# An audio tower of 32 batches: both LayerNorms normalised by ScalarE with a scale and a bias per row, and the second one's variance asked for later in VectorE's step

## The reference

```python
x: (32, 256, 256); readout = x[:, :1]; other = x[:, 1:]            # 255 tokens of width 256
h = gelu(other @ W1 + readout @ W2 + b)                            # exact gelu
n = (h - mean(h)) / sqrt(var(h) + 1e-5)                            # LayerNorm 1, no affine
q, k, v = split(n @ qkv_w.T)                                       # 16 heads of 64
attn = softmax(q @ k.T / 8 + relative_position_bias)
h = h + concat_heads(attn @ v) @ o_w.T
m = (h - mean(h)) / sqrt(var(h) + 1e-5)                            # LayerNorm 2
gate, up = m @ (w_gate / 127).T, m @ (w_up / 127).T                # 768 columns each
h = h + (silu(gate) * up) @ (w_down / 127).T
```

## Time and profile before

| what | value |
|---|---|
| median of 3 runs | 1950.28 us (1949.91 to 1951.17) |
| the profiled execution's own time | 1951.19 us |
| its span, first to last instruction | 1949.3 us |
| one batch in the steady part | 57.80 us |
| PE, PEld, DVE, ACT, POOL busy | 95%, 88%, 82%, 73%, 51% of the span |
| mean granted TensorE clock | 0.988 of full speed |

### The profile page before, as it was taken

The page is one execution under the profiler, slowest core; times in us unless marked ns, Lnnn a source line. Parts: engine busy times, 40 slices in busy tenths (PEclk is TensorE's granted clock), DMA queues, the critical chain, the costliest instruction groups (busy, mean ns, idle before and its releaser), DMA issues.

```text
span 1949.3 us, 42778 instructions
## 1 busy us (share of the span) xinstructions
PE 1853.6 (95%) x15402; PEld 1725.0 (88%) x15402; DVE 1599.4 (82%) x4768; ACT 1422.6 (73%) x3810; POOL 990.2 (51%) x1295
## 2 busy tenths in 40 slices
PE   3699999999999999999999999999999999999995
PEld 1589999999999999999999999999999999999995
DVE  3488888888888888888888888888888888888884
ACT  5477777777777777777777777777777777777773
POOL 0255555455555555555555555555555545555553
PEclk9799999999999999999999999999999999999997
DMA  6100000000000000000000000000000000000000
GB/s 213 31 10 5 11 15 15 15 15 7 10 15 15 15 15 13 6 12 15 15 15 15 6 10 15 15 15 15 7 9 15 15 15 15 15 5 12 7 7 11
DMA packets 24885, 34.34 MB, mean 18 GB/s; under 512 B 2449, under 2 KB 17810, under 8 KB 24674
## 3 DMA queue, kind: packets, MB, share of 16 engines
q1 hardware_dynamic: 23906, 28.39, 4.9%
q0 software_dynamic: 768, 3.21, 0.4%
HBM read 23.17 MB, written 8.42 MB: 16 GB/s over the span
## 4 chain that ended last, share of the span: by engine, by line
PE 72%; DMA 12%; DVE 8%; issue 3%; ACT 2%; SPq 1%; POOL 0%; POOLq 0%; DVEq 0%
PE ps L484 41%; DMA out<-h 12%; PE ps L550 9%; PE ps L529 9%; PE ps L539 8%; PE ps L493 3%; PE ps L501 2%; DVE var_eps L805 1%; DVE stats L795 1%; DVE v L832 1%; DVE h L887 1%; ACT prob L716 1%; DVE heads L863 1%; DVE heads L861 1%; SPq L409 1%
## 5 line engine op out<-in xcount | busy, mean ns | idle before, releaser
L716 ACT ACTIVATE prob<-prob,neg_top 128x255 f32<-128x255 f32 x1024 | 508.3, 500 | 67.7 <-DVE neg_top L841 67.3
L442 POOL TENSOR_TENSOR prob<-prob,inv 128x510 f32<-128x510 f32 x512 | 520.3, 1037 | 68.1 <-DVE inv L855 63.9
L447 POOL CAST oT<-heads 128x256 fp32r<-128x256 f32 x256 | 105.9, 414 | 787.4 <-DVE heads L863 787.4
L484 PE MATMUL ps<-xnT,wqk 128*128 128x256 f32 x3072 | 411.6, 283 | 3.9 <-DVE qk L824 2.1
L850 DVE TENSOR_TENSOR pT<-ps,pT 128x512 fp32r<-128x512 f32 x512 | 352.0, 688 | 60.2 <-ACT pT L722 53.2
L484 PEld LDWEIGHTS ps<-xnT,wqk 128*128 128x128 f32 x3072 | 386.4, 189 | 12.2 <-DVE qk L824 2.9
L841 DVE CUSTOM_DVE_ANT_0 prob<-ps,bias 128x255 f32<-128x255 f32 x1024 | 369.6, 416 | 2.0 <-PE ps L529 1.9
L722 ACT ACTIVATE pT<-ps 128x512 fp32r<-128x512 f32 x512 | 302.8, 592 | 26.9 <-PE ps L539 25.0
L550 PE MATMUL ps<-pT,v 128*128 128x256 f32 x2048 | 295.0, 286 | 2.2 <-DVE pT L850 1.9
L550 PEld LDWEIGHTS ps<-pT,v 128*128 128x128 f32 x2048 | 265.1, 189 | 13.5 <-DVE pT L850 1.4
L539 PE MATMUL ps<-ident,prob 128*128 128x128 f32 x2048 | 265.4, 272 | 0.1
(11 more groups left out here) (93 smaller groups left out, 2479.5 us busy)
## 6 DMA issues: line engine op xcount, KB each, us to landing
xt<-x_cols SPq DMA_DIRECT2D x32, 256.0 KB, 2.7
r_rows<-readout_rows SPq DMA_DIRECT2D x32, 128.0 KB, 3.1
out<-h SPq DMA_DIRECT2D x32, 128.0 KB
out<-h SPq DMA_DIRECT2D x32, 127.0 KB
flipped<-bias_rows POOLq DMA_DIRECT2D x1, 3072.0 KB, 16.5
staged<-w_qk SPq DMA_DIRECT2D x8, 256.0 KB, 5.0
staged<-w_v SPq DMA_DIRECT2D x4, 256.0 KB, 7.3
staged<-w_o SPq DMA_DIRECT2D x4, 256.0 KB, 3.1
```

The lines of the kernel that those rows point to most:

```text
L442: pool.tensor_tensor(pr, pr, by, ALU.mult).then_inc(prob_done, 1)
L484: mm = pe.matmul(dst, lhs(a, k), rhs(b, k), start=(start and n == 0), stop=(stop and n == last), skip_group_check=skip)
L716: ex = act.activation(pr, pr, ACT.Exp, bias=neg_top[:, g % 2, hh, t:t + 1], scale=-1.0, accum_out=total[:, g % 2, hh, t:t + 1])
```

## The change

- `normalise` moves from VectorE to ScalarE. It becomes an activation with the function Identity, a scale per row (`rstd`) and a bias per row, for each of the two tiles. So for each LayerNorm two tensor_scalar of 128x256 leave VectorE and two activations of 128x256 come to ScalarE.
- The bias is minus the mean times `rstd`. VectorE negates the mean in place (a new tensor_scalar over 128x2 in `layer_var`, ahead of the one that adds epsilon). GpSimd multiplies it by `rstd`, behind its power, and writes the product over `var_eps` (a new tensor_tensor over 128x2, behind a wait for the power through the new semaphores `ln_pow`).
- On ScalarE `normalise(1, i-1)` stands in step 3 and `normalise(0, i+1)` in step 4, both between `heads_moved` and `probs_hi` of the first head of pair G-1.
- On VectorE `layer_var(1, i-1)` moves in step 3 from its place ahead of `values_lo` of group 2 to a place behind `probs_lo` of the second head, ahead of `queries_keys_lo`.
- The short description of the change also says that the fourth value group becomes the late user of step 3. The diff has no line of that kind: `V_EARLY`, `V_LATE`, `V_GROUP` and TensorE's order stay as they are.

```diff
@@ names of semaphores
+        ln_pow = [sem(f"ln{n}_pow") for n in (1, 2)]
@@ GpSimd, layer_norm
                     pool.wait_ge(ln_var[n], count(1, batch))
                     pool.tensor_tensor(rstd[:, n, :], var_eps[:, n, :], minus_half[:], ALU.pow
+                                       ).then_inc(ln_pow[n], 1)
+                    pool.wait_ge(ln_pow[n], count(1, batch))
+                    pool.tensor_tensor(var_eps[:, n, :], mean_var[:, n, :, 0], rstd[:, n, :], ALU.mult
                                        ).then_inc(ln_rstd[n], 1)
@@ ScalarE
+                def normalise(n, batch, src):
+                    act.wait_ge(ln_rstd[n], count(1, batch))
+                    for t in range(TT):
+                        ins = act.activation(normed[:, t, :], src[:, t, :], ACT.Identity,
+                                             bias=var_eps[:, n, t:t + 1], scale=rstd[:, n, t:t + 1])
+                    ins.then_inc(ln_done[n], 1)
@@ ScalarE, step
                     if pair(G - 2):
                         heads_moved(*pair(G - 2))
+                    if g == 3 and i > 0:
+                        normalise(1, i - 1, h1)
+                    if g == 4 and nxt:
+                        if prev:
+                            act.wait_ge(lnT_mm[1], count(1, i - 1))
+                        normalise(0, i + 1, token_tile(i + 1))
                     if pair(G - 1):
                         probs_hi(*pair(G - 1), 0)
 
                 gelu(0)
+                normalise(0, 0, token_tile(0))
@@ VectorE, layer_var
                     dve.wait_ge(ln_aggr[n], count(1, batch))
+                    dve.tensor_scalar(mean_var[:, n, :, 0], mean_var[:, n, :, 0], -1.0, None, ALU.mult)
                     dve.tensor_scalar(var_eps[:, n, :], mean_var[:, n, :, 1], EPS, None, ALU.add
                                       ).then_inc(ln_var[n], 1)
-
-                def normalise(n, batch, src):
...
@@ VectorE, step
-                    if g == 3 and i > 0:
-                        layer_var(1, i - 1)
                     if gu_at(G - 1, GU_LATE):
                         gating(*gu_at(G - 1, GU_LATE))
                     if v_at(G - 1, V_LATE):
                         values_lo(*v_at(G - 1, V_LATE))
                     if pair(G - 2):
                         probs_lo(*pair(G - 2), 1)
+                    if g == 3 and i > 0:
+                        layer_var(1, i - 1)
@@ VectorE, step, further down
-                    if g == 3 and i > 0:
-                        normalise(1, i - 1, h1)
...
-                    if g == 4 and nxt:
-                        if prev:
-                            dve.wait_ge(lnT_mm[1], count(1, i - 1))
-                        normalise(0, i + 1, token_tile(i + 1))
@@ VectorE, ahead of the steps
                 layer_var(0, 0)
-                normalise(0, 0, token_tile(0))
```

## The result

The changed kernel takes 1973.56 us (median of 4 runs, 1972.45 to 1974.01) against 1950.72 us for the kernel before in the same session: a ratio of 1.0116, with a 95% interval of 1.0099 to 1.0134. It is 1.2% slower. The forecast was 1973.5. The profiled span grew from 1949.3 to 1972.1 us, 22.8 against 23.2 in the sum of the prediction. The median of before was 1950.28 when the forecast was made and the runs of one kernel spread by 1.6 us, so an error of 0.1 us is finer than these times can show.

A forecast was written before the change was run, and what follows sets the result against it. TensorE, working 95% of the span, bounds the kernel, with one wait of 26.0 us for value group 2. Terms: 30 x 0.71 = 21.3, plus 0.2 and 1.7 for the ends, together 23.2: 1973.5 against 1950.28, range 1944 to 1982.

The forecast's parts named there:

- The bound and its cause: Step 3: TensorE waits 0.83 us ahead of values(i, 3), as VectorE's L805 waits for GpSimd; 26.0 us in all.
- The hold moves with the operation: Step 3: the wait for GpSimd moves from ahead of values(i, 3) to ahead of queries_keys_lo, starting at about 1013.20.
- The rival in which the hold vanishes: Step 3: neither 128x2 operation is held, queries_keys_lo starts near 1012.6; 0.30 us a batch, 1961; chance 10%.
- The price of a pair: Two normalising activations on ScalarE: 586 ns each, one holding the engine 0.49 us, a pair 0.98.
- The walk: Start times followed along VectorE and ScalarE through steps 3 and 4; gate_up(i-1, 1) and the next batch 0.71 us later.
- 4s - 1.25: Delay of a batch for s held by one normalisation: 0.71 us at 0.49, 0.39 at 0.41, 0 at 0.31.
- The ends: Both ends of the program, where LayerNorm's path is open: 0.85 us each, 1.7 for both.
- What I would have seen: Profile after: L832 wait gone, hold about 0.75 us, pair held 0.98, three new TensorE waits, a batch of 58.5 us.
- the three waits: TensorE in each batch: for pT in step 4, for hnT, for gated ahead of gate_up(i-1, 1); 0.5 us or more.
- The faster rival: Steps 3 and 4: ScalarE's idle time pays for the pairs, 1926; chance 15%, faster with mixtures 19%.
- Operands per row that cost nothing: ScalarE's activation takes 414 ns, 0.32 held: 0.03 us a batch, 1953, no change; chance 8%.
- Table reloads: Identity in another table: loads of 1.283 us, four a batch, 5.1 us more, near 2130; chance 2%.

The follow-up runs named there:

- the move alone: Kernel before with only layer_var(1) moved in step 3, normalising stays on VectorE: 1929.83 us, ratio 0.9895 to the kernel before.
- The kernel in which it was made to vanish: Changed kernel with layer_var(1) further back in VectorE's step 3, behind add_bias: 1962.79 us, ratio 1.0071 to the kernel before.
- The three lengths of the activation: Changed kernel, and it with the activation as a copy with only the scale per row, or a plain copy: 1973.56, 1961.07, 1950.05 us.
- ScalarE's normalising alone: Changed kernel with layer_var(1) back at its old place in step 3: 1990.29 us, ratio 1.0204 to the kernel before.

## Why the prediction was right

- **The bound and its cause.** One wait of TensorE in step 3, made by a 128x2 operation that waits for GpSimd. Shown: with the operation elsewhere the 0.83 us are gone. The 0.97 us are 0.78 in the move alone, where GpSimd is still multiplying, and 0.17 where VectorE normalises and the variance stands behind `add_bias`.
- **The hold moves with the operation.** Foretold: `queries_keys_lo` at 1013.20 by the walk, 0.09 us earlier than before. Measured 1013.17 (1023.80 less 10.63). The rival in which the hold vanishes would have given 1961. The kernel in which it was made to vanish gives 1962.8.
- **The price of a pair.** Foretold 586 ns each and 0.98 us held; measured 591 and 0.98.
- **The walk.** Foretold and measured, less 10.63: `probs_hi` 1017.05 and 1017.02; `queries_keys_lo` of pair 5 1019.75 and 1019.71; tanh 1025.06 and 1025.02; gating 1025.47 and 1025.42. `gate_up(i-1, 0)` was to be 0.2 us late and is 0.20, `gate_up(i-1, 1)` 0.71 and is 0.69 (1026.35 against 1025.66). A batch was to be 0.71 us longer and is 0.69.
- **4s - 1.25.** The three lengths of the activation give a slope of 3.9 to 4.0. The second constant holds too: at 0.31 us held the batch is about as long as before (57.74 against 57.79).
- **The ends.** Foretold 0.85 us each. At the start the way from the aggregation to TensorE's transposes is 2.94 us instead of 2.24, so 0.70: GpSimd's multiplication takes 0.19 us, not the 0.35 that I took. At the end it is 2.83 us instead of 2.14, so 0.69. Together 1.4 and not 1.7. This is the one term that was off, and it is small. The parts as named also add to 0.87 each, where I wrote 0.85, and the chances named one by one to 98%. With the measured terms the sum is 30 x 0.69 + 0.2 + 1.4 = 22.3, against 22.8 in the span.
- **What I would have seen.** The pair, the hold, the batch and the three waits came as told. Each of the three was to be 0.5 us or more; as idle time of the matmuls they are 0.42, 0.36 and 0.24. The size was right for the weight loads alone (20.0, 19.5 and 16.7 us over some 31 batches, 0.54 to 0.65 each), as a matmul's idle time begins later, at the modelled end of the one before. Together the three are 1.02 us, just above the 1 us under which I had called myself wrong.
- **The faster rival** (ScalarE hides it all) had more in its favour than the prediction counted. Of the gap in step 4 it named only the 0.17 us ahead of the exp; 0.79 more lie ahead of the copy of `hnT` in the kernel before:

```profile
1019.96 0.60 ACT L698 ACTIVATE hnT<-ps 128x512 fp32r<-128x512 f32 x1 [0.79 <-PE ps L501]
```

  In the changed kernel that copy comes without a wait and the whole gap, 1.07 us, stands behind it. The rival fell because the pairs stood beside that gap and not in it; with one of them in it some seven tenths of the loss went.
- **The other rivals.** Operands per row that cost nothing fall by the 405, 497 and 591 ns. Table reloads fall by the count: ScalarE loads a table 32 times at the exp, 32 times at the gelu and once in the setup, before and after.

## What to carry to other kernels

When TensorE is bound by a round trip through two other engines, the cost of moving work is read from the stretch between two of its waits: in these runs an operation counted in full where its engine runs without a break inside the trip, and much less in the gap next to it. Ask of each idle time what ends it, and put moved work ahead of that. A change of two parts is worth taking apart, for here one part gained 21 us and the other lost 39. Look at the longest duration of a tiny VectorE operation beside its median: 974 and 776 against 171 ns here meant a wait for GpSimd. Moving it behind what the next engine waits for brought 21 us, and moving it on to a time when GpSimd is done another 7 to 8 us.

## What the runs showed of the hardware

An activation of 128x256 took 405 ns with no operand per row, 497 with one and 591 with two; with the second the function changed too, from Copy to Identity. GpSimd's 128x2 multiplication took 0.19 to 0.20 us where its 128x2 power took 0.69. A 128x2 tensor_scalar in place, with a step of two elements, was held beside GpSimd's multiplications as was the one with a packed output: up to 974 ns (ScalarE's normalising alone) against 168, and up to 974 against 169. Of two such operations in a row only the first was held (0.77 and 0.15 us).
